# ScalarE's loop of six heads one head later, and the order of a tile's first maxima piece in an attention and expert kernel

## The chip, the cores and the metric

The kernel runs on one core of a Trainium2 chip, as one program. The metric is the device time of one execution in microseconds. Before the change it is 3489.64 us, the median of three runs (3488.87 to 3498.64).

## The reference

The input is 4 sequences of 2048 tokens with 256 features. They are normalised, and two results are added to the input: attention with 16 heads of 16 features, and a mixture of 16 experts. Only the attention is touched by the change:

```python
q, k, v = (xn @ W.T + b for W, b in ((Wq, bq), (Wk, bk), (Wv, bv)))   # 16 heads of 16
scores = einsum('bqhd,bkhd->bhqk', q * SCALE, k)
probs = softmax(scores.astype(float32), axis=-1)
out = einsum('bhqk,bkhd->bqhd', probs, v) @ Wo.T + bo
```

With 4 sequences and 16 heads there are 64 (sequence, head) pairs. The kernel and this text call each of them a head.

## The kernel before, in words

The kernel has four stages: `norm`, `project`, `attend` and `finish`. The change is in `attend`, which takes some 2700 us of the span. Each engine there has an instruction stream of its own, written out by hand, and the streams meet only at semaphores.

A head is worked in two passes. The first finds the largest score of each query. TensorE multiplies 128 queries by 512 keys twice into one buffer `m_ps` (`pass1`, L770, called with k = 0 and k = 1), and this makes one piece of 1024 keys. VectorE reduces the piece to its maximum (L851). There are 32 pieces to a head and two buffers, so that `pass1` with k = 0 waits on the semaphore `maxed` for VectorE to have finished the piece two before. After 32 pieces VectorE makes `row_max` (L853); ScalarE and GpSimd split it in two, VectorE transposes it, and SyncE puts it as two more rows into the queries.

The second pass computes the scores with keys on the partitions, in 16 tiles of 128 keys, kt = 0 to 15. A tile has five scores of 512, 512, 512, 256 and 256 queries (`score`, L780, j = 0 to 4), ScalarE's exponential of each (`exp`, L724), and `weigh` (L789), four pairs of matmuls that weigh the values with the exponentials of two tiles earlier. Scores go through three buffers `s_ps`: score n waits on `exped` for the exponential n - 3. TensorE's order in one tile is

```
score 0, first piece k=0, score 1, first piece k=1, score 2, weigh, score 3, second piece k=0, score 4, second piece k=1
```

The pieces belong to the next head or, from kt = 11, to the one after it. The first pass uses rows 0 to 47 of TensorE's array and the scores use rows 64 to 113, so that one of each can run side by side; `weigh` uses all rows. ScalarE also has two small jobs in each head: it copies the finished head's sums out (`collect`, L736, after the third exponential of kt = 1) and rounds the next head's maxima (`round_shift`, L731, at kt = 12).

Each engine's stream over the heads is a loop of ten rounds with six heads written out in it (`nc.Fori`, U = 6, ROUNDS = 10), with the rest of the heads written out before and after. TensorE's and ScalarE's loops both take heads 1 to 60, so both jump back between heads 6 and 7, 12 and 13, and so on to 54 and 55: nine jumps each. SyncE's loop also jumps there. VectorE runs ahead, and its nine jumps fall at kt = 11 of heads 7, 13, ..., 55. In the code written out before and after the loops, semaphore values are constants; inside the loops they are computed in registers, by further instructions.

Of the kernel before, what the change touches and what calls it, by code (L numbers as in the profile page):

```python
# [48 lines left out]
HEADS = B * H  # L49
# [437 lines left out]
def attend(nc, sem, sb, ps, t):  # L487
    R = 3
    U = 6
# [11 lines left out]
    ROUNDS = (HEADS - 4) // U  # L501
# [49 lines left out]
    def slot(g, kt, j):  # L551
        return g * SLOTS + kt * NP + j

    def cols(j):
        return slice(CUTS[j], CUTS[j + 1])

    def wide(j):
        return slice(0, CUTS[j + 1] - CUTS[j])

    def tile(g, kt):  # L560
        return g * ST + kt

    with nc.Block() as block:
# [148 lines left out]
        @block.scalar  # L712
        def _(act):
            act.sem_inc(exped, R)
            act.sem_inc(att_read, 1)
            act.wait_ge(ones_set, 1)
            for u in range(2):
                act.activation(k_feat[u][96:P, :], prob[0][96:P, :], ACT.Copy).then_inc(ones_made, 1)

            def exp(g, r, kt, j):  # L720
                if j == 0:
                    act.wait_ge(weighed, tile(g, kt) + 1)
                act.wait_ge(scored, slot(g, kt, j) + 1)
                act.activation(prob[tile(r, kt) % R][:, cols(j)], s_ps[slot(r, kt, j) % R][:, wide(j)],  # L724
                               ACT.Exp).then_inc(exped, 1)

            def round_shift(n, r):
                if not (isinstance(n, int) and n == 0):
                    act.wait_ge(shift_turned, n)
                act.wait_ge(row_maxed, n + 1)  # L730
                act.activation(shift[:, 0, :], row_max[r % R][:, :], ACT.Copy).then_inc(shift_rounded, 1)  # L731

            def collect(g):
                act.wait_ge(weighed, tile(g + 1, 0) + R)
                act.wait_ge(att_out, (g + 1) * 16)
                act.activation(att[:, :], a_ps[:, :], ACT.Copy).then_inc(att_read, 1)  # L736

            def step(g, r, first=False, following=True):
                for kt in range(ST):
                    for j in range(NP):  # L740
                        exp(g, r, kt, j)
                        if following and (kt, j) == (ROUND_AT, 2):
                            round_shift(g + 1, r + 1)
                        if not first and (kt, j) == (LAG - 1, 2):
                            collect(g - 1)

            round_shift(0, 0)
            step(0, 0, first=True)
            with nc.Fori(0, ROUNDS, engines=[ENGINE.Activation], hint_back_edge=True) as i:
                for r in range(1, U + 1):  # L750
                    step(i * U + r, r)
            for g in range(1 + ROUNDS * U, HEADS):
                step(g, g, following=g + 1 < HEADS)
            collect(HEADS - 1)

        @block.tensor
        def _(pe):
            pe.sem_inc(weighed, R)

            def wait_fed(n_r, it, done):  # L760
                pe.wait_ge(done[n_r % 2], (it * (U // 2) + n_r // 2 + 1) * 16 * LOADS)

            def pass1(n, it, r, p, k):
                if k == 0:
                    if p == 0:
                        wait_fed(r, it, fed_low)
                    pe.wait_ge(maxed, n * PAIRS + p + 1)
                qt, half = divmod(p, 2)
                key = half * 2 * BLK + k * BLK
                ins = pe.matmul(m_ps[p % 2][:, k * BLK:(k + 1) * BLK], q_feat[r % 2][LOW, qt * P:(qt + 1) * P],  # L770
                                k_feat[r % 2][LOW, key:key + BLK], start=True, stop=True)
                if k == 1:
                    ins.then_inc(piece, 1)

            def score(g, it, r, kt, j):
                if (kt, j) == (0, 0):
                    wait_fed(r, it, fed_up)
                    pe.wait_ge(shift_in, (g + 1) * 16 * SHIFT_LOADS)
                pe.wait_ge(exped, slot(g, kt, j) + 1)
                pe.matmul(s_ps[slot(r, kt, j) % R][:, wide(j)], k_feat[r % 2][UP, kt * P:(kt + 1) * P],  # L780
                          q_feat[r % 2][UP, cols(j)], start=True, stop=True).then_inc(scored, 1)

            def weigh(g, r, kt):
                if kt == 0:
                    pe.wait_ge(v_ready, g + 1)
                    pe.wait_ge(att_read, g + 1)
                pe.wait_ge(exped, slot(g, kt, NP - 1) + 1 + R)
                for qb in range(QB):
                    ins = pe.matmul(a_ps[qb * VW:(qb + 1) * VW, :], v_head[r % R][:, kt, :],  # L789
                                    prob[tile(r, kt) % R][:, qb * BLK:(qb + 1) * BLK],  # L790
                                    start=(kt == 0), stop=(kt == ST - 1))
                ins.then_inc(weighed, 1)

            def step(g, it, r, first=False, following=True, after=True):
                def half(kt, k):
                    p = 2 * kt + EARLY + k
                    if p < PAIRS and following:
                        return lambda j: pass1(g + 1, it, r + 1, p, j)
                    if p >= PAIRS and after:
                        return lambda j: pass1(g + 2, it, r + 2, p - PAIRS, j)  # L800
                    return lambda j: None

                for kt in range(ST):
                    a, b = half(kt, 0), half(kt, 1)
                    score(g, it, r, kt, 0)
                    a(0)
                    score(g, it, r, kt, 1)
                    a(1)
                    score(g, it, r, kt, 2)
                    if kt >= LAG:  # L810
                        weigh(g, r, kt - LAG)
                    elif not first:
                        weigh(g - 1, r - 1, ST + kt - LAG)
                    score(g, it, r, kt, 3)
                    b(0)
                    score(g, it, r, kt, 4)
                    b(1)

            for p in range(PAIRS):
                for k in range(2):  # L820
                    pass1(0, 0, 0, p, k)
            for p in range(EARLY):
                for k in range(2):
                    pass1(1, 0, 1, p, k)
            step(0, 0, 0, first=True)
            with nc.Fori(0, ROUNDS, engines=[ENGINE.PE], hint_back_edge=True) as i:
                for r in range(1, U + 1):
                    step(i * U + r, i, r)
            for g in range(1 + ROUNDS * U, HEADS):
                step(g, 0, g, following=g + 1 < HEADS, after=g + 2 < HEADS)  # L830
            for kt in range(ST - LAG, ST):
                weigh(HEADS - 1, HEADS - 1, kt)
# [509 lines left out]
```

## Time and profile before

| | |
|---|---|
| median of three runs | 3489.64 us |
| the profiled execution, its own time | 3480.91 us |
| its span, first to last instruction | 3479.2 us |
| mean granted TensorE clock | 0.974 of full speed |
| busy: TensorE, VectorE, ScalarE, GpSimd | 95%, 83%, 73%, 27% |

The profile is of one execution. Busy shares are averages over the four stages, and overlapping matmuls make TensorE's share larger than what it computes at full rate. A row of a timeline gives start, length, engine, line, operation, its output and inputs, how many instructions were merged and, in brackets, how long the engine was idle before it and which instruction ended this idle time ("issue" is none that the profile shows).

### The profile page before, as it was taken

To read this page: it belongs to the slowest core of one execution; us is meant where nothing else is said; L and a number is where in the kernel's file an instruction comes from. 1 tells how busy PE (TensorE), PEld (TensorE's weight loads), DVE (VectorE), ACT (ScalarE), POOL (GpSimd) and SP (SyncE) were. 2 spreads that over 40 slices of the span, in tenths; PEclk is the share of its full clock that TensorE was granted. 3 is DMA by queue.
4 is the path that set the end of the run, shared out by engine and by line. 5 is a ranking of instruction groups with operands and counts; after the bars stand their busy time and mean duration, and the time that the engine had idled before them with its cause. 6 is when DMAs were issued, how large, how long until landed. Compare 5 with 4: busy or idle time off the path is not lost. (4 is left out here: it accounts for less than half of the span.)

```text
span 3479.2 us, 74610 instructions
## 1 busy us (share of the span) xinstructions
PE 3313.0 (95%) x20848; PEld 1662.5 (48%) x20848; DVE 2895.0 (83%) x2987; ACT 2528.7 (73%) x5726; POOL 931.4 (27%) x1339
## 2 busy tenths in 40 slices
PE   7869999999999999999999999999999999599998
PEld 6423444444444444444444444444444444288887
DVE  7508999898998999998998998998998998267777
ACT  3552888888888888887888888888887888543433
POOL 2550222222222222222222222222222222144443
PEclk9986999999999999999999999999999999899999
DMA  6680112122111111111121111221111111355553
GB/s 198 178 233 31 50 53 57 52 61 58 54 56 56 53 56 54 53 53 53 53 58 54 56 55 54 59 58 54 56 54 53 53 53 47 113 136 163 163 165 115
DMA packets 133063, 272.29 MB, mean 78 GB/s; under 512 B 22512, under 2 KB 68656, under 8 KB 120432
## 3 DMA queue, kind: packets, MB, share of 16 engines
q1 hardware_dynamic: 130464, 266.68, 26.6%
q8 instruction: 176, 2.88, 0.4%
q10 hardware_dynamic: 2256, 1.36, 0.1%
q14 instruction: 167, 1.37, 0.1%
HBM read 173.59 MB, written 84.93 MB: 74 GB/s over the span
## 5 line engine op out<-in xcount | busy, mean ns | idle before, releaser
L851 DVE TENSOR_REDUCE half_max<-m_ps 128x1 f32<-128x1024 f32 x2048 | 2414.2, 1220 | 359.9 <-PE m_ps L770 344.8
L724 ACT ACTIVATE prob<-s_ps 128x512 f32<-128x512 f32 (+1 forms) x5120 | 2190.2, 521 | 459.7 <-PE s_ps L780 439.6
L780 PE MATMUL s_ps<-q_feat,k_feat 50*128 50x512 f32 (+1 forms) x5120 | 1548.7, 399 | 28.5 <-ACT prob L724 21.1
L770 PE MATMUL m_ps<-k_feat,q_feat 48*128 48x512 f32 x4096 | 1441.5, 455 | 54.8 <-DMA k_feat<-k_parts 28.3
L780 PEld LDWEIGHTS s_ps<-q_feat,k_feat 50*128 50x128 f32 x5120 | 800.8, 185 | 1063.7 <-ACT prob L724 931.6
L789 PE MATMUL a_ps<-prob,v_head 128*32 128x512 f32 x8192 | 1099.0, 609 | 0.0
L770 PEld LDWEIGHTS m_ps<-k_feat,q_feat 48*128 48x128 f32 x4096 | 684.1, 188 | 286.1 <-DVE half_max L851 246.6
L579 POOL TENSOR_TENSOR shift<-row_max,shift 128x16 fp32r<-128x16 f32 x64 | 14.3, 223 | 1236.0 <-ACT shift L731 1236.0
L789 PEld LDWEIGHTS a_ps<-prob,v_head 128*32 128x32 f32 x8192 | 161.4, 108 | 255.4 <-issue 206.9
L1133 ACT ACTIVATE g_hi<-g 128x512 fp32r<-128x512 f32 x128 | 81.0, 632 | 243.4 <-DVE g L1171 200.5
L1296 POOL TENSOR_TENSOR g_lo<-g,g_hi 128x512 fp32r<-128x512 f32 x128 | 173.2, 1353 | 229.8 <-ACT g_hi L1133 229.8
L606 POOL TENSOR_SCALAR step_of<-route,cand 64x256 f32<-64x256 f32 x217 | 199.0, 917 | 44.5 <-POOL held L607 38.3
L573 POOL COPY v_head<-v_all 128x256 f32 (+1 forms) x64 | 25.4, 398 | 671.8 <-PE a_ps L789 671.7
L607 POOL TENSOR_TENSOR held<-held,step_of 64x256 f32<-64x256 f32 x217 | 157.8, 727 | 39.8 <-POOL step_of L606 39.8
L1171 DVE TENSOR_TENSOR g<-g,mask_bc 128x512 f32<-128x512 f32 x128 | 133.5, 1043 | 35.8 <-ACT g L1130 30.5
L1066 PE MATMUL o_ps<-w_hi,g_hi 128*128 128x256 f32 x512 | 145.6, 284 | 6.8 <-issue 4.4
L1066 PE MATMUL o_ps<-w_lo,g_hi 128*128 128x256 f32 x512 | 145.2, 284 | 0.0
L1066 PE MATMUL o_ps<-w_hi,g_lo 128*128 128x256 f32 x512 | 144.0, 281 | 0.0
L1055 PE MATMUL h_ps<-xn_hi,w_hi 128*128 128x512 f32 x256 | 105.2, 411 | 31.8 <-DMA b_rows<-b_parts 31.8
L1130 ACT ACTIVATE g<-h_ps,b_col 128x512 f32<-128x512 f32 x128 | 86.2, 674 | 26.5 <-PE h_ps L1055 26.5
L1066 PEld LDWEIGHTS o_ps<-w_hi,g_hi 128*128 128x128 f32 x512 | 97.3, 190 | 12.7 <-issue 7.8
L1055 PE MATMUL h_ps<-xn_hi,w_lo 128*128 128x512 f32 x256 | 101.1, 395 | 0.0
(132 smaller groups left out, 1905.7 us busy)
## 6 DMA issues: line engine op xcount, KB each, us to landing
q_feat<-q_parts SPq DMA_DIRECT2D x128, 256.0 KB
k_feat<-k_parts SPq DMA_DIRECT2D x128, 256.0 KB
q_parts<-parts SPq DMA_DIRECT2D x32, 512.0 KB, 4.7
k_parts<-parts SPq DMA_DIRECT2D x32, 512.0 KB, 4.8
q_feat<-q_parts SPq DMA_DIRECT2D x128, 128.0 KB
k_feat<-k_parts SPq DMA_DIRECT2D x128, 128.0 KB
att_dram<-att SPq DMA_DIRECT2D x64, 256.0 KB, 14.1
mask_bc<-mask_b SPq DMA_DIRECT2D x128, 128.0 KB, 4.5
```

The costliest lines, as they stand in the source:

```text
L606: do(pool.tensor_scalar(step_of[:, :], t["route"][:, c * PART:(c + 1) * PART], bound, None, ALU.is_ge))
L607: do(pool.tensor_tensor(held[:, :], held[:, :], step_of[:, :], ALU.add))
L724: act.activation(prob[tile(r, kt) % R][:, cols(j)], s_ps[slot(r, kt, j) % R][:, wide(j)], ACT.Exp).then_inc(exped, 1)
L770: ins = pe.matmul(m_ps[p % 2][:, k * BLK:(k + 1) * BLK], q_feat[r % 2][LOW, qt * P:(qt + 1) * P], k_feat[r % 2][LOW, key:key + BLK], start ...
L780: pe.matmul(s_ps[slot(r, kt, j) % R][:, wide(j)], k_feat[r % 2][UP, kt * P:(kt + 1) * P], q_feat[r % 2][UP, cols(j)], start=True, stop=Tru ...
L789: ins = pe.matmul(a_ps[qb * VW:(qb + 1) * VW, :], v_head[r % R][:, kt, :], prob[tile(r, kt) % R][:, qb * BLK:(qb + 1) * BLK], start=(kt == ...
L851: dve.tensor_reduce(half_max[r][:, p // 2, p % 2:p % 2 + 1], m_ps[p % 2][:, :], AX.X, ALU.max).then_inc(maxed, 1)
L1055: ins = pe.matmul(h_ps[e % 2][:, :], w, v, start=(c == 0 and k == 0), stop=(c == KC - 1 and k == 2))
L1066: ins = pe.matmul(o_ps[k], v, w[:, e, :], start=(e == 0 and m == 0), stop=False)
L1130: act.activation(g[e % 2][:, :], h_ps[e % 2][:, :], ACT.Gelu, bias=b1_col[:, e:e + 1]).then_inc(gelu, 1)
L1171: dve.tensor_tensor(g[e % 2][:, :], g[e % 2][:, :], mask_bc[q % 2][:, e % QTR, :], ALU.mult).then_inc(gated, 1)
L1296: pool.tensor_tensor(g_lo[e % 2][:, :], g[e % 2][:, :], g_hi[e % 2][:, :].bitcast(F32), ALU.subtract).then_inc(split, 1)
```

## The change

There are two edits, both in `attend`. On ScalarE, head 1 is written out before the loop and the loop takes heads 2 to 61, so that it jumps back between heads 7 and 8, 13 and 14, ..., 55 and 56. On TensorE, the two halves of a tile's first piece stand next to each other, ahead of score 1.

```diff
@@ ScalarE
             round_shift(0, 0)
             step(0, 0, first=True)
+            step(1, 1)
             with nc.Fori(0, ROUNDS, engines=[ENGINE.Activation], hint_back_edge=True) as i:
-                for r in range(1, U + 1):
+                for r in range(2, U + 2):
                     step(i * U + r, r)
-            for g in range(1 + ROUNDS * U, HEADS):
+            for g in range(2 + ROUNDS * U, HEADS):
                 step(g, g, following=g + 1 < HEADS)
@@ TensorE
                     score(g, it, r, kt, 0)
                     a(0)
+                    a(1)
                     score(g, it, r, kt, 1)
-                    a(1)
                     score(g, it, r, kt, 2)
```

No instruction is added or taken away in what TensorE, VectorE, GpSimd and SyncE execute. ScalarE executes the same exponentials; head 1 now has constants for its waits.

## Rows read from the trace of the kernel before

**Rows 1.** The page, costliest group (busy us, mean ns | idle before, releaser).
```profile
L851 DVE TENSOR_REDUCE half_max<-m_ps 128x1 f32<-128x1024 f32 x2048 | 2414.2, 1220 | 359.9 <-PE m_ps L770 344.8
```

**Rows 2.** Timeline of TensorE, one tile of head 28.
```profile
1506.35 0.38 PE L780 MATMUL s_ps<-q_feat,k_feat 50*128 50x256 f32 x1
...
1506.99 0.50 PE L770 MATMUL m_ps<-k_feat,q_feat 48*128 48x512 f32 x1
1507.21 0.50 PE L780 MATMUL s_ps<-q_feat,k_feat 50*128 50x512 f32 x1
1507.33 0.40 PE L770 MATMUL m_ps<-k_feat,q_feat 48*128 48x512 f32 x1
1507.55 0.43 PE L780 MATMUL s_ps<-q_feat,k_feat 50*128 50x512 f32 x1
1507.90 1.06 PE L789 MATMUL a_ps<-prob,v_head 128*32 128x512 f32 x8
1508.90 0.38 PE L780 MATMUL s_ps<-q_feat,k_feat 50*128 50x256 f32 x1
```

**Rows 3.** Timelines of weight loads, ScalarE and VectorE in the same tile.
```profile
1507.48 0.18 PEld L780 LDWEIGHTS s_ps<-q_feat,k_feat 50*128 50x128 f32 x1
...
1506.77 0.66 ACT L724 ACTIVATE prob<-s_ps 128x256 f32<-128x256 f32 x2 [0.42 <-PE s_ps L780]
...
1504.58 2.36 DVE L851 TENSOR_REDUCE half_max<-m_ps 128x1 f32<-128x1024 f32 x2 [0.19 <-PE m_ps L770]
```

**Rows 4.** Timeline of TensorE in head 63, which has no pieces in its tiles.
```profile
2976.00 1.07 PE L789 MATMUL a_ps<-prob,v_head 128*32 128x512 f32 x8
...
2978.55 1.06 PE L789 MATMUL a_ps<-prob,v_head 128*32 128x512 f32 x8
```

**Rows 5.** Timeline of ScalarE: `collect` in steps 18, 19 and 20.
```profile
1074.28 0.60 ACT L736 ACTIVATE att<-a_ps 128x512 f32<-128x512 f32 x1
...
1115.52 0.60 ACT L736 ACTIVATE att<-a_ps 128x512 f32<-128x512 f32 x1
...
1161.82 0.60 ACT L736 ACTIVATE att<-a_ps 128x512 f32<-128x512 f32 x1
```

**Rows 6.** Timeline of ScalarE after a jump back, from the first loop instructions.
```profile
1111.55 3.82 ACT L724 ACTIVATE prob<-s_ps 128x512 f32<-128x512 f32 x8 [0.19 <-PE s_ps L780]
...
1119.49 1.85 ACT L724 ACTIVATE prob<-s_ps 128x256 f32<-128x256 f32 x4 [3.10 <-issue]
```

**Rows 7.** Waits of ScalarE from 430 to 2900 us (total, times, longest).
```profile
ACT prob L724 <- issue: 18.8, 7, 3.3
```

**Rows 8.** Window after that stall; the granted clock stands behind the counts.
```profile
1120.70:1124.10 3.40, 3.40 (x17) 1.49 (x9) 0.88 (x1) 2.15 (x6) 0.00 (x0) 0.50 0.12 48
```

**Rows 9.** Instruction packets, windows 1103.9:1104.6, 1117.7:1118.2 and 1145.9:1146.8.
```profile
q14 instruction: 1, 0.01, 4.7%
...
q14 instruction: 1, 0.01, 3.9%
...
q14 instruction: 1, 0.01, 3.6%
```

**Rows 10.** Timeline of VectorE at its jump back in head 19.
```profile
1145.93 3.49 DVE L851 TENSOR_REDUCE half_max<-m_ps 128x1 f32<-128x1024 f32 x3 [0.72 <-issue]
```

**Rows 11.** Timelines of VectorE and TensorE, head 20 at kt = 11 and 12.
```profile
1186.85 0.19 DVE L853 TENSOR_REDUCE row_max<-half_max 128x16 f32<-128x32 f32 x1
...
1188.32 0.50 PE L770 MATMUL m_ps<-k_feat,q_feat 48*128 48x512 f32 x1 [0.22 <-DVE half_max L851]
1188.40 0.49 PE L780 MATMUL s_ps<-q_feat,k_feat 50*128 50x512 f32 x1
...
1188.73 0.38 PE L780 MATMUL s_ps<-q_feat,k_feat 50*128 50x512 f32 x1
```

**Rows 12.** Timelines of TensorE and its weight loads before head 0 (clock 0.50).
```profile
262.55 0.79 PE L770 MATMUL m_ps<-k_feat,q_feat 48*128 48x512 f32 x1 [0.18 <-DVE half_max L851]
...
262.55 0.50 PEld L770 LDWEIGHTS m_ps<-k_feat,q_feat 48*128 48x128 f32 x2 [0.90 <-DVE half_max L851]
```

## The prediction

> **What bounds the kernel now.** I read the page first. Its largest group is VectorE's reduction of the pieces, and nearly all of the idle time before it is a wait for TensorE's piece [rows 1]; so VectorE is busy, and yet not the last to be waited for. I then took the timelines of one tile in the middle of a head. The reader is to see a closed chain there. Score 3 starts at 1506.35 [rows 2] and ScalarE begins its exponential 0.42 us later, at 1506.77; the exponentials of scores 3 and 4 end at 1507.43, and the weights of score 2, which needs the buffer of exponential 4, load at 1507.48 [rows 3]. Score 2 starts at 1507.55, `weigh` at 1507.90, and the next score 3 at 1508.90, which closes the chain [rows 2]: 0.42 + 0.66 + 0.05 + 0.07 + 0.35 + 1.00 = 2.55 us a tile. No piece of the first pass is a link of it. Head 63 has no pieces and the same 2.55 us from `weigh` to `weigh` [rows 4], so that a tile is set by scores, exponentials and `weigh` alone. VectorE, two reductions of together 2.36 us with 0.19 us idle [rows 3], is close behind.
>
> Then I looked for tiles that take longer, by the times of `collect`, which stands once in each head. From step 18 to step 19 there are 41.24 us and from 19 to 20 there are 46.30 us [rows 5]. Between the last two lies a jump back of both loops. ScalarE runs five and three more exponentials, its copy and one exponential of the new round, and then stands for 3.10 us with "issue" as the cause [rows 6]. The list of waits has 7 of these, 18.8 us in total [rows 7]; the other two of the nine are shorter (1.5 and 1.3 us) and are booked on TensorE there. TensorE goes idle with ScalarE, and after it comes back the granted clock is 0.50, which is the 1.2 GHz level, for 3.4 us [rows 8]. It was at the full level before, and had stood still for nearly all of the stall.
>
> **ScalarE's loop, moved by one head.** Taking the distances of all 63 `collect` copies as in [rows 5], the nine heads with the stall exceed 41.12 us by 40.6 us together. VectorE's own jump in the same heads accounts for 0.72 us each [rows 10], 6.6 us. The other 34.0 us are stall and low clock, and are what this edit can win.
>
> Whether it does depends on what the stall is. It isn't the jump itself, for the stall comes 4.8 us after the new round's first exponential (1119.49 - 3.10 - 1111.55) [rows 6]. An 8 KB instruction packet arrives at 1117.8, during the stall, and ScalarE goes on 1.7 us later; VectorE also has such a packet after its jump, at 1146.3, 0.3 us after its first reduction [rows 9, 10], and has no stall further on. So I take it that a jump asks for the block after its target, and that ScalarE's loop begins shortly before the end of a block and uses it up before the next one is there. The compiled loop has 1084 instructions; the stall stands 25 instructions into it. ScalarE needs 41.1 us for the 180 instructions of a head, and its packets are 29.3 us apart where nothing disturbs them, 128 instructions. Head 1 written out with constants is 100 instructions (80 exponentials, 16 waits on `weighed`, 4 for `collect` and `round_shift`). The loop's start therefore moves from 25 to 53 instructions before a block's end (25 - 100 + 128), which is 12 us instead of 5.5 us after the jump at 1110.9. The packet at 1117.8 came 6.9 us after the jump, and the instructions could be used 8.6 us after it. 12 us covers that, and I cost this stall at nothing, with the first four tiles of the new round as its cover.
>
> The same shift moves the loop's end. Today the last block is entered 34 instructions before the jump, and a packet follows at 1104.0 [rows 9], 6.9 us before the jump, which I read as the target's block. After the change the last block is entered only 6 or 7 instructions, about 1.7 us, before the jump. From entering a block to its use I count 1.3 us to the packet and 1.7 us from there [rows 6, 9], 3.0 us. ScalarE may thus stand 1.3 us at the jump; 0.42 us of idle time in each tile [rows 3] and the buffered scores take part of it. I take 0.7 us for each of nine jumps: +6 us. The bounds are nothing and a stall as long as today's, 34 us.
>
> What I read of the Trainium skill, "Runtime: NRT & Kernel Launch", section "Instruction fetch mechanics", is that a taken branch to a target outside a small window must first fetch the target's page, so that the stall would stand at the branch. In the trace it stands 5.5 us behind the jump at 1110.9. By the rule alone the stall would only move with the loop, and the time would stay.
>
> **The two halves side by side.** This changes all tiles with a piece, some 990. Where the chain is the one above, piece half 0 starts at 1506.99, when VectorE has released its buffer, and score 1 at 1507.21, when exponential 3 is through [rows 2]. With its weights loaded behind that release, the first half streams from about 1507.10; 512 columns take 0.21 us, so half 1 can start at 1507.31. Score 1 with its weight load of 0.1 us is ready to stream at 1507.31 as well, and uses other rows. Score 2 stays where exponential 4 puts it. The cost in such a tile is nothing; the cover is exponential 4, and if score 1 came later than 1507.37 it would be gone (1507.58, where score 2 streams, less 0.21). The first piece is complete 0.02 us earlier, which VectorE can't use: it is still reducing the other one. I see no tile where this order gains more.
>
> It costs where VectorE is late. At kt = 12 of each head VectorE has done `row_max` as well, the first half waits until 1188.32, and score 1 starts 0.08 us after it [rows 11]. After the change score 1 stands behind half 1, which starts 0.32 us after half 0: 1188.64. Score 2 would be at 1188.86 rather than 1188.73 [rows 11], 0.13 us later, and this shift is passed on by `weigh` to the next tile. 61 heads make +8 us. Bounds: nothing, if the next tile regains it, and 0.2 us each, 12 us.
>
> The skill, "TensorE: Matmul & The Clock Gate", section "Part 3: Packing small matmuls — row/col tiling", says that a weight load overlaps a running matmul only if it goes to another row group. Half 1 would then load its weights after half 0 has ended. This trace speaks against it: before head 0, two loads for the same rows are done within 0.50 us, while the first matmul, begun with the first of them, runs for 0.79 us [rows 12]. A sum by the rule is that of the second rival.
>
> **Sum.** -34 + 6 + 8 = -20 us. The profiled execution would go from 3480.9 to 3461 us. The median of three is 8.7 us above the profiled execution, and I keep this distance: 3489.6 - 20 = 3469.6, and I say 3470 us.
>
> **Rivals.**
> (1) The stall only moves. If ScalarE asks for the next block when it comes near its end, or if the target's block at the end of the loop costs as much as today's stall, the 34 us stay and the order costs up to 8: 3490 to 3498 us. For it: in all nine rounds the packet comes about when the 25 instructions are used up. Against it: VectorE's packet, 0.3 us after the jump's end. Price per round is up to 3.8 us.
> (2) The order costs in every tile, on the other side of my forecast. The place is score 1. If its weights can't be loaded ahead of a waiting half 1, it streams at 1507.42 instead of 1507.31 (0.50 us with the load against 0.39 us without, in [rows 2, 11]), and score 2 at 1507.63 instead of 1507.58. 0.05 us in 990 tiles are 50 us; with the loop's gain of 28 and kt = 12 the time is 3489.6 - 28 + 8 + 50 = 3520 us. It decides from 0.02 us a tile on, where it has used up the 20 us. For it: a wait stands in front of score 1's load. Against it: score 0 today stands behind half 1 of the second piece and starts with it.
> (3) The stall goes and neither the loop's end nor kt = 12 costs anything: 3489.6 - 34 = 3456 us.
> (4) The edit of the order does nothing, the loop gains 28: 3462 us; this lies in my forecast's own range.
>
> **How the numbers follow.** Forecast 0.50 (with (4), own range 3460 to 3479), (1) 0.22, (2) 0.15, (3) 0.13. 0.3% of 3490 us is 10.5 us, and about what a measurement of this kernel tells from no change. Faster than 3479: the forecast, (3), less the forecast's upper edge, and a mild form of (1): 0.62. Within 10.5 us: most of (1) and a mild (2): 0.21. Slower: the bulk of (2) and a tail of (1): 0.17. The range reaches from (3), with 3 us below it, to the upper end of (1) and a little above: 3453 to 3502 us. It leaves out most of (2).
>
> **What would show it.** Right: `collect` to `collect` over the heads 7, 13, ... falls from 46.3 to some 42 us; no ScalarE wait of over 2 us with "issue" in `attend`; no window at clock 0.50 after a jump; tiles of 2.55 us with score 2 still 0.07 us behind its weight load; at kt = 12 score 1 about 0.3 us behind half 0. A stall of 3 us some 12 us after ScalarE's jump, or one at the jump itself, would be (1). Tiles of 2.60 us, with score 1 more than 0.35 us behind half 0, would be (2). The forecast is also wrong if TensorE, whose jump stays, has a stall of its own that ScalarE's has hidden.

## The result and the profile after

| | before | after |
|---|---|---|
| median, four runs each on one chip | 3494.14 us (3488.87 to 3511.31) | 3446.19 us (3444.21 to 3446.53) |
| profiled execution, its own time | 3480.91 us | 3444.21 us |
| its span | 3479.2 us | 3442.4 us |
| mean granted TensorE clock | 0.974 | 0.978 |

The ratio is 0.9853, with a 95% interval of 0.9817 to 0.9889. The kernel became 48 us (1.5%) faster, where I had said 20 us; 3446 us lies below my range, which began at 3453. From `pass1` on, line numbers are one higher than before.

The stall at ScalarE's jump is gone. The timeline of ScalarE after the change, with the `collect` copies of two steps; the jump is at 1143.3:

```profile
1106.14 0.60 ACT L736 ACTIVATE att<-a_ps 128x512 f32<-128x512 f32 x1
...
1143.15 0.66 ACT L724 ACTIVATE prob<-s_ps 128x256 f32<-128x256 f32 x2 [0.42 <-PE s_ps L781]
1144.01 3.82 ACT L724 ACTIVATE prob<-s_ps 128x512 f32<-128x512 f32 x8 [0.20 <-issue]
1147.96 0.60 ACT L736 ACTIVATE att<-a_ps 128x512 f32<-128x512 f32 x1
1148.46 2.12 ACT L724 ACTIVATE prob<-s_ps 128x256 f32<-128x256 f32 x5
1151.01 2.13 ACT L724 ACTIVATE prob<-s_ps 128x256 f32<-128x256 f32 x5 [0.43 <-PE s_ps L781]
```

From `collect` to `collect` there are 41.82 us, against 46.30 in the same place before [rows 5]. The exponentials that followed 3.10 us of idle time before [rows 6] now follow at once, and those of the next tile wait 0.43 us for TensorE, as in any tile. Nor is there a wait at the jump itself. The waits of ScalarE from 430 to 2900 us say it for all rounds, 1.2 us in place of 18.8 [rows 7]:

```profile
ACT prob L724 <- PE s_ps L781: 379.3, 951, 1.0
ACT prob L724 <- issue: 1.2, 5, 0.3
```

With the stall went the low clock. The window over the twelve microseconds behind the jump, granted clock 1.00 behind the counts, where [rows 8] had 0.50 (over the whole stretch from 430 to 2900 us it is 1.00, before 0.99):

```profile
1144.01:1156.00 11.99, 11.99 (x82) 5.40 (x82) 11.01 (x10) 10.58 (x24) 6.52 (x9) 1.00 0.32 83
```

The instruction packets stand in windows 1141.9:1142.4 and 1148.8:1149.3. ScalarE enters the last block of the loop, 7 instructions ahead of the jump, 1.7 us before it. The packet that follows this entry comes 1.2 us before the jump, and the next one 5.7 us after the jump (before they came 6.9 us ahead of it and 6.9 us after it [rows 6, 9]). The second packet of the first window isn't ScalarE's: it comes there in after + 28 below as well, where ScalarE's own packet comes 6.9 us before the jump.

```profile
q14 instruction: 2, 0.02, 10.1%
...
q14 instruction: 1, 0.01, 3.9%
```

Between the two profiled executions the span differs by 36.8 us. The nine heads with a jump, by their `collect` copies, took 410.6 us and take 376.8: 33.9 us less before rounding. The other 2.9 us are spread over the first stage, the tail and the other heads, 1.1 us at most in one place. What the two profiles don't show is where the rest of the 48 us comes from; the experiments do.

In the tiles nothing moved. TensorE in an ordinary tile, and at kt = 12 of head 20:

```profile
1171.60 0.50 PE L771 MATMUL m_ps<-k_feat,q_feat 48*128 48x512 f32 x1
1171.82 0.50 PE L781 MATMUL s_ps<-q_feat,k_feat 50*128 50x512 f32 x1
1171.94 0.39 PE L771 MATMUL m_ps<-k_feat,q_feat 48*128 48x512 f32 x1
1172.16 0.43 PE L781 MATMUL s_ps<-q_feat,k_feat 50*128 50x512 f32 x1
1172.52 1.07 PE L790 MATMUL a_ps<-prob,v_head 128*32 128x512 f32 x8
...
1173.85 0.39 PE L781 MATMUL s_ps<-q_feat,k_feat 50*128 50x512 f32 x1
1174.46 0.50 PE L771 MATMUL m_ps<-k_feat,q_feat 48*128 48x512 f32 x1 [0.22 <-DVE half_max L852]
1174.55 0.49 PE L781 MATMUL s_ps<-q_feat,k_feat 50*128 50x512 f32 x1
1174.80 0.39 PE L771 MATMUL m_ps<-k_feat,q_feat 48*128 48x512 f32 x1
1174.89 0.39 PE L781 MATMUL s_ps<-q_feat,k_feat 50*128 50x512 f32 x1
1175.21 0.64 PE L790 MATMUL a_ps<-prob,v_head 128*32 128x512 f32 x4
```

The gaps of the ordinary tile (0.22, 0.12, 0.22 us) are those of before [rows 2]. That the new order is what ran, the weight loads of this tile show. Those of the two halves now stand together, the second at 1171.71, ahead of score 1's; before, half 1's stood behind score 1's:

```profile
1171.60 0.29 PEld L771 LDWEIGHTS m_ps<-k_feat,q_feat 48*128 48x128 f32 x2 [0.22 <-DVE half_max L852]
1171.82 0.18 PEld L781 LDWEIGHTS s_ps<-q_feat,k_feat 50*128 50x128 f32 x1
```

Half 1's load also runs while half 0 computes (1171.60 to 1172.10), though both use the same rows of the array, as I had read from [rows 12]. The kt = 12 rows are the surprise. TensorE's compiled stream is score 0, half 0 with its wait on `maxed`, half 1, score 1, score 2. In the trace score 0 starts at 1173.85, half 0 at 1174.46 when VectorE lets it, **score 1 at 1174.55 and half 1 at 1174.80**. Score 1 stands behind half 1 in the stream and starts 0.25 us ahead of it. It starts 0.09 us behind half 0, where I had said 0.3, and before it was 0.08 [rows 11]. The ordinary tile has the same inversion, score 1 at 1171.82 and half 1 at 1171.94. From `weigh` to `weigh` the tile at kt = 12 takes 2.69 us, against 2.68 before.

### The profile page after: what moved, and what is told of

Its sections match the earlier page's. It is cut to its first block and busy times, and to the rows that moved or that the text cites. A ratio compares the mean times of both kernels' runs of the same rounds, so it can differ in the third digit from the quotient of the medians.

```text
span 3442.4 us, 74610 instructions
## 1 busy us (share of the span) xinstructions
PE 3296.2 (96%) x20848; PEld 1706.4 (50%) x20848; DVE 2894.2 (84%) x2987; ACT 2526.4 (73%) x5726; POOL 929.1 (27%) x1339
## 5 line engine op out<-in xcount | busy, mean ns | idle before, releaser
L771 PE MATMUL m_ps<-k_feat,q_feat 48*128 48x512 f32 x4096 | 1405.1, 448 | 55.9 <-DMA k_feat<-k_parts 28.4
L771 PEld LDWEIGHTS m_ps<-k_feat,q_feat 48*128 48x128 f32 x4096 | 616.3, 187 | 287.5 <-DVE half_max L852 248.6
L1056 PE MATMUL h_ps<-xn_lo,w_hi 128*128 128x512 f32 x256 | 102.1, 399 | 0.0
```

What stands on the lines that cost most here:

```text
L1056: ins = pe.matmul(h_ps[e % 2][:, :], w, v, start=(c == 0 and k == 0), stop=(c == KC - 1 and k == 2))
```

## The experiments

ScalarE's compiled stream is cut here into blocks of 128 instructions, the size of its packets. For each kernel I give two distances: how many instructions the loop's start lies before the end of its block, and how many instructions of the last block stand before the jump. They are 24 and 35 in the kernel before, 52 and 7 after (the prediction counted one more at the start). The compiled stream doesn't tell where the first block begins in memory: I set this so that the stall of the kernel before stands at a block's end. The packets then fit the count in all kernels but two, which are named below: each entry into a block is followed by one packet, in the kernel after 0.5 to 5.3 us later. To move the loop without touching what it does, some kernels have more instructions at the start of ScalarE's part of `attend`, each of which only counts up an unused semaphore:

```diff
             act.sem_inc(att_read, 1)
+            for _ in range(PADS):
+                act.sem_inc(pads, 1)
```

All results (PADS over before or after; interval 95%; the ratios are to the kernel before on the same chip, median 3498.0 us in the first group, 3483.6 in the second, 3487.3 in the third):

| group | kernel | start, jump | us | ratio |
|---|---|---|---|---|
| 1 | loop edit alone | 52, 7 | 3446.2 | 0.9853 (0.9832 to 0.9873) |
| 1 | order edit alone | 24, 35 | 3499.8 | 1.0005 (0.9992 to 1.0017) |
| 1 | before + 100 | 52, 7 | 3451.8 | 0.9867 (0.9843 to 0.9891) |
| 1 | after + 28 | 24, 35 | 3497.9 | 0.9992 (0.9965 to 1.0019) |
| 2 | before + 21 | 3 by count | 3445.1 | 0.9877 (0.9851 to 0.9904) |
| 2 | before + 114 | 38, 21 | 3443.6 | 0.9875 (0.9849 to 0.9901) |
| 2 | after + 121 | 59, 0 | 3538.8 | 1.0150 (1.0123 to 1.0177) |
| 2 | before, once more | 24, 35 | 3486.8 | one run |
| 3 | before + 12 | 12 by count | 3443.6 | 0.9882 (0.9860 to 0.9904) |
| 3 | after + 124 | 56, 3 | 3518.5 | 1.0106 (1.0073 to 1.0139) |
| 3 | jump inside a head, + 78 | 24, 35 | 3445.6 | 0.9888 (0.9868 to 0.9909) |

**One edit at a time.** The first kernel has only the edit of ScalarE's loop, the second only that of TensorE's order.

> Only ScalarE's loop is moved; TensorE's order is that of before. Theory A (the loop's place is the whole gain, the order is worth nothing): a profile of 3442 to 3445 us, a time within 0.15% of the changed kernel's, no ScalarE wait of over 2 us with 'issue' in attend. Rival B (the order brings a part): it is slower than the changed kernel by that part, 3450 us or more.

> Only the order of the halves is changed; ScalarE's loop is that of before. Theory A: like before within what its own runs scatter, a profile of 3475 to 3490 us, with the nine stalls; the tile at kt = 12 still takes 2.68 us, because score 1 starts ahead of the waiting second half although it stands behind it. Rival B: faster than before by more than 10 us.

The loop edit has the ratio of the whole change, to the fourth digit, and the order edit is at one within 0.17%. With the order alone the nine stalls are as before, though its profiled execution took 3515.7 us, above the 3475 to 3490 that I expected. Its ScalarE timeline and two windows behind the same round's jump at 1116.7:

```profile
1121.81 0.38 ACT L724 ACTIVATE prob<-s_ps 128x256 f32<-128x256 f32 x1
1125.14 1.86 ACT L724 ACTIVATE prob<-s_ps 128x256 f32<-128x256 f32 x4 [2.95 <-issue]
```

```profile
1121.00:1124.40 3.40, 1.74 (x12) 0.89 (x8) 3.11 (x3) 1.05 (x3) 0.40 (x1) 1.00 0.46 137
1124.70:1138.40 13.70, 12.83 (x52) 5.43 (x52) 5.56 (x5) 7.80 (x17) 0.00 (x0) 0.50 0.13 53
```

A stall of 2.95 us, no longer than the 3.10 us of [rows 6], was followed by 13.7 us at the low level, where the first profile had 3.4 us [rows 8]. This is the missing part of the gain, and the next kernel looks at it.

**The kernel before, profiled again.**

> The kernel before, for a second profile. Nine stalls of ScalarE 5.5 us after its jumps. If the profile shown before had short stretches at the low clock by luck, this one has more than 3.4 us at clock 0.50 behind some of them, and a span of 3485 us or more.

Its windows at clock 0.50, for two of the nine rounds:

```profile
1112.20:1119.00 6.80, 6.36 (x26) 2.17 (x26) 2.44 (x3) 4.20 (x9) 0.00 (x0) 0.50 0.17 67
1617.30:1631.00 13.70, 12.20 (x51) 5.21 (x52) 5.16 (x6) 7.38 (x17) 0.00 (x0) 0.50 0.13 53
```

Over the nine heads, and less VectorE's 6.5 us, stalls and low clock took 43.0 us in this execution. In the first profile it was 34.0 us, with the order alone 66 us. The executions' own times follow: 3480.9 us for 34.0, 3486.8 for 43.0, 3515.7 for 66. The kernel before scatters for this reason: its 23 runs in the first group lie between 3488 and 3512 us, while the four of after lie within 2.3 us. The time of these 23 runs goes with their mean granted clock, from 0.970 in the fastest to 0.962 in the slowest. The first profile had 0.974 and a shorter time than all 23, so it was a lucky draw.

**The place in the block, or the heads that jump together?** After the change ScalarE jumps one head later than TensorE, so that the two no longer jump in the same moment. That could be the cure as well. One kernel gives ScalarE the block position of after, with its jumps where they were (before + 100). The other one gives it the position of before, with the jumps a head apart (after + 28).

> The kernel before, with 100 one-instruction semaphore increments on ScalarE at the start of attend, where ScalarE has nothing to do. Its loop still takes heads 1 to 60 and jumps together with TensorE's, but every instruction of the loop lies 100 further on, as in the changed kernel. Theory A (what counts is how many instructions lie between the loop's start and the end of its block, 24 before and 52 here): the stall is gone, 3442 to 3450 us. Rival B (what counts is that ScalarE and TensorE jump at the same time and fetch at the same time): the nine stalls stay, 3475 us or more.

> The changed kernel, with 28 one-instruction semaphore increments on ScalarE at the start of attend. ScalarE still jumps one head after TensorE, but its loop starts 24 instructions before the end of a block, as in the kernel before. Theory A: stalls of 1.5 to 3.5 us come back, in heads 8, 14, ..., some 5 us after ScalarE's jump, and the time is 25 to 40 us above the changed kernel's. Rival B: no stall, the time of the changed kernel.

The position decides whether there is a stall. Before + 100 has none of the nine. After + 28 has all nine again, of 1.3 to 1.9 us, and the whole gain is lost. Its ScalarE timeline behind the jump at 1151.5, the packet in window 1156.6:1157.1 and the clock behind it:

```profile
1152.20 3.83 ACT L727 ACTIVATE prob<-s_ps 128x512 f32<-128x512 f32 x8 [0.19 <-issue]
1156.16 0.60 ACT L739 ACTIVATE att<-a_ps 128x512 f32<-128x512 f32 x1
1156.66 0.38 ACT L727 ACTIVATE prob<-s_ps 128x256 f32<-128x256 f32 x1
1158.68 1.85 ACT L727 ACTIVATE prob<-s_ps 128x256 f32<-128x256 f32 x4 [1.64 <-issue]
```

```profile
q14 instruction: 1, 0.01, 5.4%
```

```profile
1160.30:1170.50 10.20, 10.20 (x47) 4.94 (x43) 5.15 (x5) 5.98 (x14) 8.25 (x11) 0.50 0.26 80
```

It is the instruction that stalls in [rows 6], one head later: ScalarE has used its 24 instructions 5.5 us behind the jump, the packet comes 5.3 us behind it, and the next instruction starts 1.9 us after the packet.

The length of the stall is another matter. Where ScalarE's jump stands alone (after, loop edit alone, after + 28) the packet came 4.8 to 5.8 us behind it in all 27 rounds. Where TensorE jumps in the same moment it came 4.8 to 7.1 us behind it, and the stalls of the kernel before reach 3.3 us. Jumping together may thus lengthen a stall, but it doesn't make one.

Before + 100 is 5.7 us slower than the loop edit alone, and 2 us above what I expected of it. It has one stall that the other one has not, behind the loop's last exit, in head 62 which is written out:

```profile
2884.88 0.66 ACT L727 ACTIVATE prob<-s_ps 128x256 f32<-128x256 f32 x2 [0.43 <-PE s_ps L783]
2888.17 2.13 ACT L727 ACTIVATE prob<-s_ps 128x512 f32<-128x512 f32 x5 [2.64 <-issue]
```

```profile
2889.70:2903.40 13.70, 13.70 (x57) 5.95 (x56) 7.93 (x7) 8.06 (x20) 0.00 (x0) 0.50 0.03 11
```

The head takes 48.28 us instead of 41. By the count the stall stands where the block that holds the exit ends, 120 instructions behind the exit. After + 28 and after + 121 have a long last head, head 63, with 61.2 and 56.8 us where nearly all the other kernels have 38.2. In after + 28 it ran at clock 0.50 for 68.3 us from 2962.6 on. Its median came out 52 us above that of after, where I had expected 25 to 40 us; of the 71 us between the two profiled executions the nine heads make 41 and the last head 23.

**How many instructions are enough?** Three kernels put the loop's start 38, 12 and 3 instructions before a block's end.

> The kernel before with 114 increments: the loop starts 38 instructions before the end of a block, some 8.5 us of ScalarE's work. Theory A: the packet comes 4.8 to 7 us after the jump and the instructions are there at 6.5 to 8.7 us, so no stall in most rounds and a short one, under 0.5 us, in some; within 15 us of the changed kernel. Rival C: the packet comes at 8 us or later, with stalls of 1.5 to 3 us as in the kernel before.

> The kernel before with 21 increments on ScalarE at the start of attend: its loop starts 3 instructions before the end of a block. Theory A, as the last four runs left it (a jump asks for the block behind its target, its packet comes 4.8 to 7 us after the jump wherever the loop lies, and can be used 1.7 us later): ScalarE stands right behind the jump for some 6 us in each round, and it is slower than before, 3510 us or more. Rival C (the block is asked for when its end comes near): the packet comes within 2 us of the jump, and the stall is 3 us as before.

> The kernel before with 12 increments: the loop starts 12 instructions before the end of a block, some 2.7 us of work. If the block behind the target is asked for by the jump and comes 4.8 to 7 us after it (theory A), ScalarE stands from 3 us after each jump until 6.5 to 8.7 us, 3.5 to 6 us, and the time is 20 to 60 us above the kernel before. Rival D, after the run with 3 instructions, which did not stand at all: a start this close to the block's end is fetched together with the block behind it, and there is no stall, 3445 us.

38 is enough: packets 5.0 to 7.0 us behind the jump, and no wait with "issue" over 0.3 us. But 3 and 12 have no stall either, where theory A said 3510 us or more and 20 to 60 us above the kernel before, and their packets show that my count does not hold for them. Both have the packets at the same places of the loop, nine in a round where the kernel before has ten, as if the loop began with a new block. I take it that the loaded program moves a loop's start to a block's beginning when few instructions are left in its block; this is only inferred. Those two kernels don't tell what 3 or 12 instructions would cost.

**The other end.** My sum had 0.7 us for entering the last block only 7 instructions before the jump. Two kernels enter it 3 instructions before the jump and with the jump itself.

> The changed kernel with 121 increments: the loop starts 59 instructions before the end of a block, and its jump is the first instruction of the last block, so that the target's block can't be asked for ahead of it by entering that block. If the target's block is asked for on entering the jump's block, as the prediction has it, ScalarE stands at the jump for 1.5 to 3 us in each round, 15 us or more above the changed kernel. If it is asked for earlier (or kept), there is no stall and the time is the changed kernel's.

> The changed kernel with 124 increments: its jump is the fourth instruction of the last block (eighth in the changed kernel, first in the run with 121). If entering the last block asks for the target's block, 0.7 us ahead of the jump here, and the packet needs 0.5 to 1.3 us and 1.7 us to be used, a stall of some 1 to 2.5 us stands at each jump, 10 to 40 us above the changed kernel. If a jump drops a request that is under way, the stall is the 6.5 us of the run with 121, and the time 3530 us or more.

ScalarE's timeline in after + 121, jump at 1157.3, and in after + 124, jump at 1157.8:

```profile
1156.77 0.66 ACT L727 ACTIVATE prob<-s_ps 128x256 f32<-128x256 f32 x2 [0.42 <-PE s_ps L784]
1163.69 2.13 ACT L727 ACTIVATE prob<-s_ps 128x512 f32<-128x512 f32 x5 [6.26 <-issue]
```

```profile
1157.61 0.66 ACT L727 ACTIVATE prob<-s_ps 128x256 f32<-128x256 f32 x2 [0.42 <-PE s_ps L784]
1164.00 2.14 ACT L727 ACTIVATE prob<-s_ps 128x512 f32<-128x512 f32 x5 [5.74 <-issue]
```

The waits of ScalarE with "issue", in the same order:

```profile
ACT prob L727 <- issue: 60.0, 9, 7.3
```

```profile
ACT prob L727 <- issue: 48.8, 9, 5.7
```

The packets of after + 121 in window 1157.4:1167:

```profile
q14 instruction: 2, 0.02, 0.4%
```

Here the stall stands at the jump, 6.7 and 5.4 us in the mean, and both kernels are slower than the one before. The first packets come 4.5 and 4.3 us behind these jumps, ScalarE goes on 1.9 us after each, and a second packet follows at 9.2 and 9.0 us. In the kernel after there is one packet 1.2 us ahead of the jump and one behind it. The queue has 15 packets a round in all three kernels. So the packet isn't one more, it is the same one, later: entering the last block asks for the block of the jump's target, and the jump has to wait for it where it isn't there. This is inferred from the packets' places and their number, for the trace doesn't show what a packet holds. At 7 instructions it costs nothing, because it is there in time. At 3 instructions the last block is entered only 0.2 us ahead of the jump, too late. But the 4.3 us that the packet then takes are far more than the 0.5 us behind the entry at 7 instructions. Of my two readings for after + 124, 1 to 2.5 us of stall and 6.5 us, neither came true, and the 5.4 us are nearer to a request that the jump drops. Between 7 and 3 there is a cliff that no sum of mine has.

**A jump in the middle of a head.** The packet of the block behind the loop's start comes 4.8 to 7.1 us behind the jump in the kernels without a stall at the jump. In the last one ScalarE's loop begins and ends at kt = 8, with 24 instructions before the block's end.

```diff
+            step(1, 1, kts=(0, 8))
             with nc.Fori(0, ROUNDS, ...) as i:
                 for r in range(1, U + 1):
-                    step(i * U + r, r)
+                    step(i * U + r, r, kts=(8, ST))
+                    step(i * U + r + 1, r + 1, kts=(0, 8))
```

> The kernel before with ScalarE's loop begun in the middle of head 1 (at kt = 8), so that it jumps in mid-head, away from SyncE's loads at the start of a head and from TensorE's jump, and with 78 increments, so that it starts 24 instructions before the end of a block, as in the kernel before. If the late packet (4.8 to 7 us after the jump) comes from the loads at the start of a head, the packet here comes 1 to 2 us after the jump and there is no stall: 3445 us. If it is ScalarE's jump itself that takes this long, the packet still comes at 4.8 us or later and the stalls of 1.3 us or more stay.

Its ScalarE timeline behind the jump at 1121.0:

```profile
1121.70 3.82 ACT L727 ACTIVATE prob<-s_ps 128x512 f32<-128x512 f32 x8 [0.20 <-issue]
1125.95 2.27 ACT L727 ACTIVATE prob<-s_ps 128x256 f32<-128x256 f32 x5 [0.43 <-PE s_ps L786]
```

No stall with the same 24 instructions. The packet comes 3.5 to 3.9 us behind the jump here, between the 1 to 2 us and the 4.8 us or more of my two readings, and with the 1.9 us to its use seen above that is about when the 24 instructions are used up (5.5 us). What makes it 5 to 7 us at a head's start isn't shown. The transfers are a candidate: from the jump to the packet they moved 163 GB/s in the kernel before (1110.9:1117.8), 119 in the one after (1143.3:1149.0) and 53 here (1121.0:1124.7). But this kernel also moves the jump away from TensorE's, and nothing tests the transfers alone.

## Why the prediction was wrong

The chain of the tile and what the stall is were right, and the sign too. Three terms of the sum were off, all to the same side: of the 23 us between my 3469.6 and the measured 3446.2, the two costs that I added make 14, the distance from the profiled execution to the median some 7, and small differences elsewhere in the span 3.

**"-34 us": the right place, the wrong size.** The nine heads gave back 33.9 us between the two profiles, as the term says. But it was read from one execution whose low-clock stretches happened to be short. The step that failed here is "the median of three is 8.7 us above the profiled execution, and I keep this distance". This distance was itself made of the stalls: executions with 34.0, 43.0 and 66 us of them took 3480.9, 3486.8 and 3515.7 us. Beside the change the median of before is 3494.1, which is 13.2 us above the profiled one, and after the change the distance is 2.0 us. The 48 us are thus 33.9 in the nine heads, 2.9 elsewhere in the span and 11.2 of distance. Rival (3) had the right mechanism, nothing lost at either place, and missed by 10 us, most of it for this reason.

**"+6 us" at the loop's end: nothing.** The last block is entered 1.7 us before the jump, as I had it, and no round waits there. What follows the entry is the packet that the jump needs, as after + 121 and after + 124 show. The step that failed is the size: "From entering a block to its use I count 1.3 us to the packet and 1.7 us from there". The packet came 0.5 us after the entry, and 1.7 to 1.9 us behind it is 0.5 to 0.7 us after the jump, when the new round's first exponential starts anyway (0.7 us after the jump, as in the kernel before). That was luck as much as margin: the packets that follow other entries came up to 5.3 us later. My upper bound of 34 us was even too low for this place. With four instructions fewer it costs 5.4 us a round, and after + 124 is 73 to 75 us above the kernels without a stall on its chip, so that the term was a bet on a position which no row of before could decide.

**"+8 us" at kt = 12: nothing.** The step that failed here is "after the change score 1 stands behind half 1, which starts 0.32 us after half 0". In the stream it does, in the trace it doesn't. The tile grew by 0.01 us, and the edit alone gives 1.0005. Rival (2), 50 us for all tiles, falls with the same rows. What I read of the Trainium skill, "TensorE: Matmul & The Clock Gate", section "Part 3: Packing small matmuls — row/col tiling", says that matmuls start and end in program order; the rows 1174.55 and 1174.80 speak against it, for score 1 and half 1 use different rows of the array.

**Rival (1), the stall only moves: no.** The Trainium skill's rule in "Runtime: NRT & Kernel Launch", section "Instruction fetch mechanics", that a far taken branch must fetch its target before it can go on, is seen in after + 121 and after + 124 alone, where the last block is entered with the jump or 3 instructions before it. In the other kernels the target's block is there at the jump, and it is the block after it that can be late.

**What stays open:** what decides how long a packet takes, 5 to 7 us behind a jump at a head's start, 3.5 to 3.9 in its middle and 0.5 to 5.3 behind the entries into other blocks; why the target's packet takes 4.3 us when its block is asked for 0.2 us before the jump; what a loop's start with 3 or 12 instructions left does in the loaded program; why there is a stall behind the loop's exit in some kernels; and what sets the length of a low-clock stretch.

## What to carry to other kernels

Look for a wait with "issue" that comes back once in each round of a loop: count the instructions from the loop's start to its block's end and from its last block's start to the jump, and shift the loop, by idle instructions or by writing a step out, until both are far from small (here 38 of 128 at the start were enough; at the end 7 were, but 3 were not). A cheap test is the same kernel with such instructions added before the loop. And when idle time leads to low clock, the profiled execution is one draw of a cost that varies: read it in two or three executions, and take the scatter of the runs as part of what the cure will win.

## What was not expected of the hardware

- Matmuls that use different rows of the array did not start in the order of the stream: score 1 started 0.09 us after the half that had waited for VectorE, and 0.25 us before the other half, which precedes it in the stream.
- After stalls of about 3 us the granted clock stayed at 0.50 for 3.4 us in one execution and 13.7 us in another of the same loop; in after + 28, stalls of 1.3 to 1.9 us were followed by up to 17.1 us.
- Four instructions' difference in where the last block begins (7 or 3 before the jump) is worth 5.4 us of stall a round, and with the low clock behind it a ratio of 1.0106 instead of 0.9853.
